# Entering the attention of a macaron block: keys before queries, statistics of the second batch one step earlier, value products two rows at a time

## The reference

```python
x = x + 0.5 * ffn(layernorm(x), w_gate, w_up, w_down)
x = x + attn(layernorm(x), w_q, w_kv, w_proj, b_proj)
x = x + 0.5 * ffn(layernorm(x), w_gate, w_up, w_down)

# ffn:  h = silu(x @ w_gate) * (x @ w_up)     hidden width 2048
#       of every four neighbours of h the two largest |h| stay; out = h_sparse @ w_down
# attn: q = x @ w_q.T (16 heads of 32);  k, v = split(x @ w_kv.T) (one head of 32, shared by all)
#       q, k scaled by 32**-0.5 and turned by a rotary table with position scales
#       out = softmax(causal(q k^T)) v;  out @ w_proj.T + b_proj
```

## Time and profile before

| what | value |
|---|---|
| median of 3 runs | 2811.03 us (2809.7 to 2814.78) |
| the profiled execution | 2805.94 us, of which the span of the trace is 2804.1 us |
| PE busy | 2724.1 us, 97% of the span |
| DVE / ACT / POOL busy | 1862.3 / 1121.9 / 301.7 us (66 / 40 / 11%) |
| granted PE clock, mean | 0.993 |

### The profile page before, as it was taken

One profiled execution on the slowest core, in us unless ns is written; L12 is line 12 of the kernel. 1 busy time (PEld: TensorE's weight loads), 2 busy tenths in 40 slices (PEclk: granted clock), 3 DMA queues, 4 the chain that ended last, 5 costly groups with the idle time before them and its releaser, 6 DMA issues. The chain is left out here.

```text
span 2804.1 us, 41683 instructions
## 1 busy us (share of the span) xinstructions
PE 2724.1 (97%) x15520; PEld 2191.1 (78%) x15520; DVE 1862.3 (66%) x3537; ACT 1121.9 (40%) x2397; POOL 301.7 (11%) x313
## 2 busy tenths in 40 slices
PE   7999999999999998999999997999999999999998
PEld 5888888888888886677677765888888888888887
DVE  5667666765676667777777764666766766676555
ACT  3323333333233332777777773332333333233331
POOL 0000000000000005444444410000000000000000
PEclk9999999999999999999999998999999999999999
DMA  3210311121112112000000003211221122103100
GB/s 117 96 58 16 136 45 45 61 90 45 45 61 91 45 45 75 2 21 24 28 32 32 13 20 128 76 45 45 78 80 49 45 88 92 51 16 105 45 15 31
DMA packets 65165, 156.49 MB, mean 56 GB/s; under 512 B 6880, under 2 KB 7136, under 8 KB 64736
## 3 DMA queue, kind: packets, MB, share of 16 engines
q1 hardware_dynamic: 64992, 154.17, 16.3%
HBM read 128.97 MB, written 25.17 MB: 55 GB/s over the span
## 5 line engine op out<-in xcount | busy, mean ns | idle before, releaser
L368 PE MATMUL bank<-xnt_h,wgu_h 128*128 128x512 f32 x2048 | 803.8, 392 | 10.3 <-issue 7.4
L368 PE MATMUL bank<-xnt_h,wgu_l 128*128 128x512 f32 x2048 | 798.9, 390 | 0.0
L368 PE MATMUL bank<-xnt_l,wgu_h 128*128 128x512 f32 x2048 | 798.5, 390 | 0.0
L528 DVE TENSOR_TENSOR h<-bank,sg 128x512 f32<-128x512 f32 x256 | 176.8, 691 | 595.9 <-PE bank L368 580.3
L368 PEld LDWEIGHTS bank<-xnt_h,wgu_h 128*128 128x128 f32 x2048 | 385.5, 188 | 91.1 <-issue 8.7
L368 PEld LDWEIGHTS bank<-xnt_h,wgu_l 128*128 128x128 f32 x2048 | 385.4, 188 | 80.9
L368 PEld LDWEIGHTS bank<-xnt_l,wgu_h 128*128 128x128 f32 x2048 | 385.8, 188 | 79.0
L468 ACT ACTIVATE mag<-h 128x512 f32<-128x512 f32 x256 | 162.0, 633 | 702.9 <-DVE h L528 702.9
L387 PE MATMUL bank<-wd_h,hs_h 128*128 128x512 f32 x1024 | 400.0, 391 | 4.6 <-DVE hs_l L563 4.6
L387 PE MATMUL bank<-wd_l,hs_h 128*128 128x512 f32 x1024 | 399.2, 390 | 0.0
L387 PE MATMUL bank<-wd_h,hs_l 128*128 128x512 f32 x1024 | 399.1, 390 | 0.0
(11 more groups left out here) (107 smaller groups left out, 3204.0 us busy)
## 6 DMA issues: line engine op xcount, KB each, us to landing
raw_gu<-in_w_gu SPq DMA_DIRECT2D x128, 512.0 KB, 4.9
raw_d<-in_w_d SPq DMA_DIRECT2D x128, 256.0 KB, 2.6
x_mid<-x_sb SPq DMA_DIRECT2D x64, 256.0 KB, 2.0
x_sb<-in_x SPq DMA_DIRECT2D x32, 256.0 KB, 4.6
x_sb<-x_mid SPq DMA_DIRECT2D x8, 1024.0 KB, 5.5
x_sb<-x_mid SPq DMA_DIRECT2D x32, 256.0 KB, 4.8
out<-x_sb SPq DMA_DIRECT2D x32, 256.0 KB, 2.1
raw_q<-in_w_q SPq DMA_DIRECT2D x1, 1024.0 KB, 4.9
```

The costliest lines, as they stand in the source:

```text
L368: last = pe.matmul(ps, w[:, r, kind, k], xs[:, b, k], start=(i == 0), stop=(i == 3 * KD - 1))
L528: v.tensor_tensor(h[:, r], bank[UP + r % 2][:, :], sg[:, r % 2], ALU.mult).then_inc(h_done, 1)
```

## The change

The diff touches five things.

1. **Keys first (seam).** PE turns kv right after the first group of queries; DVE rotates the keys before it splits the queries; two banks are exchanged for it.
2. **Statistics of batch 1 early.** DVE takes the four `bn_stats` and the aggregation for batch 1 one step earlier (before the last `hidden`), and normalises its first two tiles inside the last `hidden`, as the other groups already do; slot 1 holds them, and POOL's `ln_gpsimd` for them comes before its wait for the last `up`.
3. **First parts of the weights by ACT.** `wkv_h` and `wq_h` are cast by ACT between its last `mag` and its four casts `hs_h`; POOL only subtracts.
4. **Paired values.** `weigh` is called only in even steps, for K-2 and then K-1; in odd steps `scores(K+3)` follows the transposes directly.
5. **Places.** `pt` keeps its eight blocks, but they go to rows by the table `PLACES` and not by K % 2.

```diff
@@ scalar step, last group @@
+                    if beside:
+                        beside()
                     for r in range(NR):
                         a.wait_ge(pruned, n * NR + r + 1)
                         a.copy(hs_h[:, b, r], h[:, r]).then_inc(hs_h_done, 1)
...
+                    step(nn + 1, 1, end, not last, lambda r: [ln_hi(a, m + NB, 0, t, bank[DOWN + t]) for t in AFTER[r]],
+                         (lambda: next(then)) if last else None)
@@ vector, last group @@
-                    if not last:
-                        for t in range(TT):
+                    for t in range(TT):
+                        if last:
+                            v.wait_ge(ax_loaded[1], 16)
+                        else:
                             v.wait_ge(x_loaded[TT + t], (g + (g0 + 2)) * 16)
                             passed(v, passed_vector)
-                            ln_stat_tile(v, 1, t, x_next(1, t))
-                        ln_aggregate(v, m + NB + 1, 1)
+                        ln_stat_tile(v, 1, t, x_next(1, t))
+                    ln_aggregate(v, m + NB + 1, 1)
...
-                        if not last and AFTER[r] and AFTER[r][-1] == TT - 1:
+                        if AFTER[r] and AFTER[r][-1] == TT - 1:
                             ln_normalise(v, m + NB + 1, 1, 0, x_next(1, 0))
                             ln_normalise(v, m + NB + 1, 1, 1, x_next(1, 1))
@@ attention @@
+            PLACES = ((7,), (5, 6), (0, 1, 2), (3, 4, 5, 6))
-            bank_of["kvt", 0], bank_of["k", 0] = bank[1], bank[2]
+            bank_of["kvt", 0], bank_of["k", 0] = bank[0], bank[1]
@@ gpsimd @@
                 ln_gpsimd(g, m0, 0)
+                ln_gpsimd(g, m0 + 1, 1)
                 g.wait_ge(up_done, LAST * NR)
-                cut_weights(0, wkv_h[:, :, :], wkv_l[:, :, :], raw_kv[:, :, :], 1)
+                g.wait_ge(aw_h_done, 1)
+                g.tensor_tensor(wkv_l[:, :, :], raw_kv[:, :, :], wkv_h[:, :, :].bitcast(F32), ALU.subtract).then_inc(aw_done, 1)
+                g.wait_ge(aw_h_done, 2)
                 for k in range(KD):
-                    cut_weights(1, wq_h[:, k], wq_l[:, k], raw_q[:, k], 2 + k)
+                    g.tensor_tensor(wq_l[:, k], raw_q[:, k], wq_h[:, k].bitcast(F32), ALU.subtract).then_inc(aw_done, 1)
...
-                finish_q(0, 0)
-                finish_q(0, 1)
-                ln_gpsimd(g, m0 + 1, 0)
-                finish_q(0, 2)
-                finish_q(0, 3)
+                for hg in range(NHG):
+                    finish_q(0, hg)
@@ tensor @@
-                    if K > 0:
+                    if k % 2 == 0 and K > 0:
+                        weigh(K - 2)
                         weigh(K - 1)
...
-                for hg in range(NHG):
-                    if hg == NHG - 1:
-                        pe.wait_ge(kvt_done, 1)
-                    project_q(0, hg)
-                pe.wait_ge(q_split, 2)
-                turn_kv(0)
-                yield
-                pe.wait_ge(q_split, 4)
+                project_q(0, 0)
+                turn_kv(0)
+                project_q(0, 1)
+                project_q(0, 2)
+                pe.wait_ge(kvtok_done, 1)
+                project_q(0, 3)
+                yield
+                pe.wait_ge(q_split, 2)
                 turn_k(0)
@@ scalar, attention @@
+                a.wait_ge(up_done, LAST * NR)
+                a.wait_ge(aw_loaded[0], 16)
+                a.copy(wkv_h[:, :, :], raw_kv[:, :, :]).then_inc(aw_h_done, 1)
+                a.wait_ge(aw_loaded[1], 16)
+                a.copy(wq_h[:, :, :], raw_q[:, :, :]).then_inc(aw_h_done, 1)
+                yield
                 drain_kv(0)
@@ vector, attention @@
-                split_q(0, 0)
-                for t in range(TT):
-                    stat(1, t)
-                split_q(0, 1)
-                ln_aggregate(v, m0 + 1, 0)
-                split_q(0, 2)
-                normalise(1, 0)
-                normalise(1, 1)
-                split_q(0, 3)
                 v.wait_ge(aw_loaded[5], 16)
                 keys(0)
+                for hg in range(NHG):
+                    split_q(0, hg)
```

More of the change, by code:

```diff
@@ L128, in macaron_kernel @@
     over(d_at, d_at)
-    pt = place("pt", [P, 2, TT, HG, P], F32)
+    pt = place("pt", [P, 2 * TT, HG, P], F32)
     over(raw_gu_at, raw_gu_at)
@@ L452, in cut_gu, with step @@
                     a.copy(wgu_h[:, r], raw_gu[:, r]).then_inc(wgu_h_done, 1)
-                def step(n, b, chunk, ahead, between=None):
+                def step(n, b, chunk, ahead, between=None, beside=None):
                     for r in range(NR):
@@ L491, in group @@
                         return
-                    step(nn + 1, 1, end, not last, lambda r: [ln_hi(a, m + NB, 0, t, bank[DOWN + t]) for t in AFTER[r]])
+                    step(nn + 1, 1, end, not last, lambda r: [ln_hi(a, m + NB, 0, t, bank[DOWN + t]) for t in AFTER[r]],
+                         (lambda: next(then)) if last else None)
                 if phase == 0:
@@ L820, in finish_q, with cut_weights @@
                     g.tensor_tensor(qt[:, B % 2, hg], qt[:, B % 2, hg], qtmp[:, n % 2], ALU.add).then_inc(q_finished, 1)
-                def cut_weights(load, h_of, l_of, raw, cut):
-                    g.wait_ge(aw_loaded[load], 16)
+                def cut_weights(h_of, l_of, raw, cut):
+                    g.wait_ge(aw_loaded[3], 16)
                     g.tensor_copy(h_of, raw).then_inc(aw_h_done, 1)
@@ L991, in weigh @@
                             last = pe.matmul(outs[s * HD:(s + 1) * HD, i * P:(i + 1) * P], kvtok[:, B % 2, j, 1],
-                                             pt[:, K % 2, j, s], start=(j == 0), stop=(j == i))
+                                             pt[:, PLACES[i][j], s], start=(j == 0), stop=(j == i))
                     if k % TT == TT - 1:
@@ L1069, in tensor @@
                     step(K)
+                weigh(ALL - 2)
                 weigh(ALL - 1)
@@ L1107, in copy_turned @@
                     a.wait_ge(p_turned, turned_by(K, j))
-                    a.copy(pt[:, K % 2, j], bank_of["p", K, j][:, :].rearrange("p (s n) -> p s n", n=P)).then_inc(pt_scalar, 1)
+                    a.copy(pt[:, PLACES[row_of(K)][j]], bank_of["p", K, j][:, :].rearrange("p (s n) -> p s n", n=P)).then_inc(pt_scalar, 1)
                 def drain_sums(G):
@@ L1170, in normalise @@
                 def normalise(B, t):
-                    ln_normalise(v, B + m0, 0, t, x_of(B, t))
+                    ln_normalise(v, B + m0, 1 if B == 1 else 0, t, x_of(B, t))
                 def lo_x(B, t):
@@ L1209, in copy_turned @@
                     v.wait_ge(p_turned, turned_by(K, j))
-                    v.tensor_copy(pt[:, K % 2, j], bank_of["p", K, j][:, :].rearrange("p (s n) -> p s n", n=P)).then_inc(pt_vector, 1)
+                    v.tensor_copy(pt[:, PLACES[row_of(K)][j]], bank_of["p", K, j][:, :].rearrange("p (s n) -> p s n", n=P)).then_inc(pt_vector, 1)
                 def invert_sums(G):
@@ L1333, in _ @@
             def _(a):
-                first_ffn[3](a, True)
-                attention[3](a)
+                then = attention[3](a)
+                first_ffn[3](a, then)
+                for _ in then:
+                    pass
             @blk.vector
```

2 lines of the change are left out of this document (1 added, 1 removed).

## The result

The changed kernel takes 2788.3 us (median of 4 runs, 2786.7 to 2788.95), the kernel before 2810.36 us (4 runs on the same chip, 2804.94 to 2814.78). The ratio is 0.9922, with a 95% interval from 0.9903 to 0.994: faster by 22 us, where 25.6 were worked out. In the profiled executions it is 2787.92 against 2805.94, so 18.0 us; that execution of before is near the lowest of its runs. The 4 us between 18 and 22 go with the clock: of nine more executions of before, five took 2811.25 to 2813.27 us at a mean granted clock of 0.990 or 0.991 and four 2805.13 to 2806.84 us at 0.993, like the profiled one, while the changed kernel had 0.992 or 0.993 in all.

A forecast was written before the change was run, and what follows sets the result against it. PE was taken to bound the kernel, busy 553.0 of 576.9 us in the loop. Seam 8.0 plus loop 17.6 gave 25.6 us off the median 2811.0, so 2785 us, range 2778 to 2799.

The forecast's parts named there:

- The hole: Seam: PE's idle before the transposes of `kwide` closes when keys come first and statistics early; gain 8.1 us.
- the low clock behind it: Seam: PE's work after the idle before `kwide`'s transposes runs at the high clock level again; gain 1.25 us.
- The new wait for `kvt`: Seam: PE's earlier `turn_kv` must wait for ACT's copy `kvt`; loss 0.8 us, bounds 0 and 1.2.
- worth nothing itself: Seam, edit 3: ACT's casts hide in its idle time and POOL finishes before the query projection; gain nothing.
- The additions of the bias: Seam: POOL's additions slow DVE's third and fourth normalised tiles, and PE waits; loss 0.5 us, bounds 0 and 0.9.
- The change of mode: Loop: each pair saves one change between 32-column and 32-row work, 0.14 us; in all 8.3 us, bounds 0 and 16.5.
- The waits for row 3's mask: Loop: row 2's `weigh` moved behind row 3's `scores` covers DVE's release of the banks; gain 8.0 us.
- the mask takes this wait back: Rival, loop: DVE is 0.3 to 0.5 us late at row 2's `scores` in 32 groups; 2798 us, chance 0.13.
- The wait for `xt_raw`: Loop, step 15 of six batches: a `weigh` of 8 records reappears inside the transposes' wait; gain 1.3 us.
- 59 x 0.14: Loop: 59 of 63 pairs each save one mode change of 0.14 us; 8.3 us, bounds 0 and 16.5.
- nothing is saved: Loop: four pairs, at steps K % 4 = 1 without a projection where `scores` waits for DVE anyway, gain nothing.
- rival for a slower kernel: Loop: the wait at row 2's `scores` grows by 1.3 us a group, long idles adding low clock; 2827 us, chance 0.04.

The follow-up runs named there:

- pool_casts: Changed kernel with edit 3 undone: GpSimd again makes the casts of the first parts of w_kv and w_q; 2788.9 us, one run.
- stats_early_keys_last: Changed kernel with the keys behind the four splits, as before the change, statistics still early; 2789.12 us, one run.
- keys_first_stats_late: Changed kernel with edit 2 undone: keys first, but batch 1's statistics and first normalised tiles back among the splits; 2785.58 us, one run.
- row1_pairs: Changed kernel with weigh paired only for rows 0 and 1; rows 2 and 3 weighed one step late as before; 2797.7 us, ratio 0.9945.
- shuffle_off_bank: Changed kernel with the query shuffle reading the product in SBUF, freeing the bank after one pass (query values wrong); 2784.93 us, one run.
- stats_sooner: Changed kernel with a batch's third and fourth statistics in steps 6 and 7 instead of 7 and 8; 2786.37 us, one run.
- pairs_only: Kernel before with edits 4 and 5 alone (paired weigh and its places); 2796.76 us, ratio 0.9945.
- row3_pairs: Changed kernel with weigh paired only for rows 2 and 3; rows 0 and 1 weighed one step late as before; 2788.21 us, ratio 0.9914.
- mixed_pairs_stats: Changed kernel, rows 0 and 1 paired only in steps 9, 10, 13, 14 from the second batch, statistics in steps 6 and 7; 2781.76 us, ratio 0.9905.
- seam_only: Changed kernel with edits 4 and 5 (the pairs) taken back, edits 1 to 3 kept; 2799.47 us, ratio 0.9953.
- changed_again: The changed kernel unaltered, timed once more beside mixed_pairs_stats on one chip; 2788.34 us, ratio 0.9925.

## Why the prediction was right, and where it wasn't

**The hole** (8.1) and **the low clock behind it** (1.25): right. The transposes of `kwide` start at 1093.65 without idle, where "near 1095" was said, and last 0.60 instead of the first 1.09 of the earlier trace rows. The keys took 1.36 us where 1.5 were given.

**The new wait for `kvt`** (0.8, bounds 0 and 1.2): mis-sized. It is 0.17, so the term is off by 0.63. The step named the reason, that GpSimd does less beside `prune`, and gave it too little; `pool_casts` gives 1.03 without it. So "worth nothing itself" of edit 3 was wrong: it is worth 0.87 us, and it acts here.

**The additions of the bias** (0.5): not there. One normalised tile does take longer beside them, 0.88 instead of 0.54 us, and PE's wait for it is 0.97 us, where before and `stats_early_keys_last` have 0.63. The next wait is shorter by as much, 2.46 for 2.80. The mechanism is real all the same: in `keys_first_stats_late` the two tiles take 1.11 and 1.53 us beside the additions, and that costs the 1.0 us above. The seam so gave 9.35 for 8.0, all of it ahead of `scores(0)`.

**The change of mode** (0.14 a pair): nearly right where nothing else acts. Steps 9 and 10 and steps 13 and 14 of `row1_pairs` save 0.15 each. With the pair of rows 2 and 3 the entry into `scores` after four transposes is 0.03 dearer than the entry into `weigh`, so 0.11 is left. Over the 31 pairs of these rows that is 0.9 us less than forecast.

**The waits for row 3's mask** (8.0): the mechanism was right. There is no wait at 384 or at 512 columns in the loop; the worked-out 3.12 us is 3.11. Steps 7 and 8 alone save 0.69. The rival that the mask takes this wait back at row 2's `scores`, "even with DVE to 0.02 us", fell: no such wait. But the forecast of "some 8 us" left of the 14.4 us of waits was too low, 10.4 are left: the four long waits grew by 1.7 us, and the five of step 9 add 1.0.

**The wait for `xt_raw`** (1.3): right. PE's waits for it went from 6.8 to 5.5 us, and step 15 is 0.22 shorter with rows 0 and 1 paired.

**The step that failed** is "59 x 0.14": that a `weigh` moved out of an odd step saves its mode change and costs nothing there. It was asked of steps without a projection only ("nothing is saved" in four of them). But row 0's `weigh`, 0.36 us, also stood before two transposes, whose bank DVE still reads in the steps with a query projection: 0.25 us twice a batch, 3.5 us over seven batches, shown by `shuffle_off_bank`. And it was the cover of step 9: row 2's `weigh`, moved ahead of row 3's, makes `att` late and with it row 3's mask, for which `scores` then waits. That is 0.25 in each of the five full batches, 1.3 in all, shown by `stats_sooner`. Per full batch the forecast comes to 8 x 0.14 for the modes, 0.5 + 2 x 0.15 for the waits and 0.22 for `xt_raw`, so 2.14 us; measured are 1.38. The two kinds of lost cover, 0.5 + 0.25, are that gap. Worked out from the steps, the 8.3 us of this term shrink to about 2.8: 28 pairs of 0.15 and 31 of 0.11, less 3.5 and 1.3.

**The remainder of the loop** is mostly the clock, some 3 us in the first batch (70.34 against the 67.16 of `pairs_only`) and 1.6 in the last two (one fall more than before). In the first batch `scores` of a step without projection waits 2.96 us and then everything behind it is slow for 5 us. PE's timeline of the changed kernel:

```profile
1153.16 0.81 PE L973 MATMUL bank<-kt,qt 32*128 32x128 f32 x8 [2.96 <-DVE nmax L1218]
1153.90 2.82 PE L982 MATMUL bank<-ident,probs 128*128 128x128 f32 x12
1156.65 1.51 PE L997 MATMUL bank<-pt,kvtok 128*32 128x128 f32 x24
```

The 24 records take 1.51 us where they take 0.86 at the high level, and the 12 transposes 2.82 for 1.53. The prediction priced these steps at "nothing saved". It didn't see that such a wait may end at 1.2 GHz. The wait is also longer than the 2.32 us of before, but no run shows that this is why the clock falls. Closer in kind was its rival for a slower kernel ("each long idle adds the 1.25 of a low clock"), which it put to another place.

That the total came near is in good part luck. The seam gave 1.35 more and the loop, at 8.2 for 17.6, less than half. Between the two profiled executions this makes 18.0 us for 25.6. The other 4 us of the measured 22 go with the lower mean clock of before's other executions, for which the sum has no term.

## What to carry to other kernels

A small piece of work that is moved out of a gap is also the cover of what stands behind it: before moving it, look in every kind of step that it leaves at which buffer the next instruction takes and who still reads it, and in the step it goes to at who waits for its result. Apply a reordering only to the steps that gain: here leaving two of a batch's eight pairs undone gains 0.25 us a batch over pairing all. When two edits shorten the same list of one engine ahead of one wait, their gains don't add; cost the second with the first in place.

## What the runs showed of the hardware that was not expected

**The clock after a wait.** In the loop TensorE falls from 2.4 to 1.2 GHz after some of its waits of 2 to 3 us and not after others. In step 9 of the first batch it falls after 2.96 us (changed kernel), 2.60 (`row3_pairs`), 2.32 (`stats_sooner`) and 1.97 (`mixed_pairs_stats`), and stays high after 2.95 (`pairs_only`), 2.68 (`row1_pairs`) and 2.32 (before). Here are the two of 2.32 us on PE's timelines, before and then `stats_sooner`, each with the 12 transposes behind the wait:

```profile
1164.22 0.50 PE L967 MATMUL bank<-kt,qt 32*128 32x128 f32 x8 [2.32 <-DVE nmax L1204]
1164.65 1.53 PE L976 MATMUL bank<-ident,probs 128*128 128x128 f32 x12
```

```profile
1154.23 0.78 PE L973 MATMUL bank<-kt,qt 32*128 32x128 f32 x8 [2.32 <-DVE nmax L1218]
1154.93 2.82 PE L982 MATMUL bank<-ident,probs 128*128 128x128 f32 x12
```

So the length of the wait alone doesn't decide; what else does was not settled. What it costs can be read from the last two batches up to the end of the output projection. Three kernels with the same lists there have no fall (`keys_first_stats_late`, 143.3 us), one (`stats_early_keys_last`, 144.8) and two (the changed kernel, 146.4). Without pairs there is one in before (148.7) and there are three in `seam_only` (151.4). That is 1.4 to 1.6 us for each fall. These were one execution each, so how often a kernel has them is open, though `changed_again` repeats the changed kernel's 70.3 and 146.4 within 0.1 us. It also means that a few microseconds of the differences between single runs are the clock and not the edit: what is said of those kernels rests on the waits and steps named, not on the totals.

**DVE beside GpSimd.** Beside GpSimd's additions DVE's copy `kwide` took 1.37 us, and it takes 0.43 alone. In `stats_early_keys_last`, where the keys stand beside GpSimd's additions again, DVE's timeline shows two operations of one size with times that differ sixfold:

```profile
1092.68 0.21 DVE L1176 TENSOR_TENSOR krot<-kvtok,rot_k 128x64 f32<-128x64 f32 x1
1092.82 1.31 DVE L1177 TENSOR_TENSOR krot<-kvtok,rot_k 128x64 f32<-128x64 f32 x1
1094.17 1.28 DVE L1194 TENSOR_TENSOR krot<-krot 128x128 f32<-128x128 f32 x1
1095.48 1.44 DVE L1198 COPY kwide<-krot 128x512 f32<-128x512 f32 x1
```

GpSimd's products and additions start at 1091.33, 1092.69, 1094.01 and 1095.38 in the trace and take 1.26 to 1.36 us each. The first row falls into the change from one to the next. The other three end 0.08, 0.15 and 0.28 us after GpSimd's instruction beside them; in the changed kernel, where GpSimd is idle at the keys, they take 0.22, 0.29 and 0.43 us. So an operation that starts just behind GpSimd's lasts 1.28 to 1.44 us, whatever its size of 64, 128 or 512 columns. The Trainium skill (page "SBUF — State Buffer", section "Who interferes with whom") says that whichever of the two engines issues first gets the shared pair of ports for the whole instruction; these rows agree, since the time is that of the partner's instruction and not of the own one.
